# Feed-forward key products in f32r parts, and a new plan for the side work of an attention loop

## The reference

```python
x = L0_attn_x                                     # 4 x 2048 x 256, f32
# attention, 16 heads of 16, 16 "splats" a head
qkv = layernorm(x) @ qkv_w.T
w(t) = exp(sum((t - centers)**2) * inv_var)       # for q and for k, per splat
logits = einsum(w(q), w(k), amplitudes) / temp
x = x + (softmax(logits) @ v) @ out_w.T
# feed-forward
h = layernorm(x); h_prev = h shifted by one token
xr = mu_r * h + (1 - mu_r) * h_prev;  xk = mu_k * h + (1 - mu_k) * h_prev
r = sigmoid(xr @ W_r.T)
k_act = square(relu(xk @ W_k.T))
x = x + r * (k_act @ W_v.T)
```

## Time and profile before

| | |
|---|---|
| median of 3 runs | 2138.8 us (2138.59 to 2140.33) |
| the profiled execution, its own time | 2140.03 us |
| its span in the trace | 2138.2 us |
| PE / PE weight loads busy | 2108.5 us (99%) / 947.4 us (44%) |
| ACT busy | 2003.9 us (94%) |
| DVE busy | 822.9 us (38%) |
| POOL busy | 398.1 us (19%) |
| first and last exponential start | 46.9 and 2103.4 us |

### The profile page before, as it was taken

One profiled execution on the slowest core, in us unless ns is written; L12 is line 12 of the kernel. 1 busy time (PEld: TensorE's weight loads), 2 busy tenths in 40 slices (PEclk: granted clock), 3 DMA queues, 4 the chain that ended last, 5 costly groups with the idle time before them and its releaser, 6 DMA issues.

```text
span 2138.2 us, 52139 instructions
## 1 busy us (share of the span) xinstructions
PE 2108.5 (99%) x22756; PEld 947.4 (44%) x22756; DVE 822.9 (38%) x1886; ACT 2003.9 (94%) x2184; POOL 398.1 (19%) x502
## 2 busy tenths in 40 slices
PE   7999999999999999999999999999999999999999
PEld 4444444444444444444444444444444444443445
DVE  6123433332436252524425225262244334514236
ACT  4999999999999999999999999999999999999995
POOL 0243342424242020220402202204000000000000
PEclk9999999999999999999999999999999999999999
DMA  6534444436533315124241421612422141221111
GB/s 196 140 94 124 120 130 127 122 90 169 126 113 98 73 61 156 34 89 118 73 136 44 125 83 49 164 36 76 110 58 55 40 90 41 44 63 34 34 41 45
DMA packets 176489, 193.59 MB, mean 91 GB/s; under 512 B 88656, under 2 KB 108496, under 8 KB 176240
## 3 DMA queue, kind: packets, MB, share of 16 engines
q1 hardware_dynamic: 166720, 174.69, 29.4%
q0 software_dynamic: 7424, 15.22, 2.9%
q10 hardware_dynamic: 2096, 0.14, 0.1%
HBM read 98.90 MB, written 75.81 MB: 82 GB/s over the span
## 4 chain that ended last, share of the span: by engine, by line
PE 79%; ACT 17%; DVE 3%; issue 1%; DMA 0%; DVEq 0%; ACTq 0%
PE ps_pv L1000 35%; PE ps_scores L981 24%; PE ps_step L1028 16%; ACT probs L1325 15%; PE ps_step L1049 1%; DVE h_t L1675 1%; ACT weight L1385 1%; PE ps_scores L1018 0%; PE ps_scores L1013 0%; PE ps_scores L1176 0%; DVE mixed_r L1660 0%; PE ps_scores L1022 0%; DMA x_prep<-x 0%; ACT gate L1382 0%; DVE gate_in L1628 0%
## 5 line engine op out<-in xcount | busy, mean ns | idle before, releaser
L1325 ACT ACTIVATE probs<-ps_scores 128x1024 f32<-128x1024 f32 x2048 | 1938.1, 1037 | 82.2 <-PE ps_scores L981 54.1
L1000 PE MATMUL ps_pv<-probs,vals 128*32 128x512 f32 (+5 forms) x9760 | 1071.8, 531 | 1.1 <-DVE o_raw L1690 1.1
L981 PE MATMUL ps_scores<-q_aug,k_aug 49*128 49x512 f32 x4096 | 707.3, 439 | 11.8 <-ACT probs L1325 7.8
L981 PEld LDWEIGHTS ps_scores<-q_aug,k_aug 49*128 49x128 f32 x4096 | 331.6, 184 | 635.5 <-ACT probs L1325 591.6
L1000 PEld LDWEIGHTS ps_pv<-probs,vals 128*32 128x32 f32 x9760 | 335.8, 139 | 208.7 <-issue 121.0
L1443 POOL DMA_DIRECT2D packed<-qk x232 | 116.9, 509 | 830.3 <-DVE qk L1617 802.7
L1448 POOL TENSOR_TENSOR packed<-qk 32x512 f32<-32x512 f32 x232 | 246.9, 1064 | 17.5
L1453 POOL TENSOR_TENSOR k_act<-k_act 128x512 f32<-128x512 f32 x28 | 29.1, 1040 | 825.0 <-DVE k_act L1620 825.0
L1690 DVE COPY o_raw<-ps_pv 128x512 f32<-128x512 f32 x63 | 43.6, 691 | 266.2 <-PE ps_pv L1000 266.0
L1617 DVE COPY qk<-ps_step 128x512 f32<-128x512 f32 x58 | 40.0, 690 | 216.6 <-PE ps_step L1028 216.4
L1620 DVE TENSOR_SCALAR k_act<-ps_step 128x512 f32<-128x512 f32 x29 | 20.0, 691 | 236.9 <-PE ps_step L1028 236.9
(11 more groups left out here) (217 smaller groups left out, 1101.7 us busy)
## 6 DMA issues: line engine op xcount, KB each, us to landing
k_aug<-k_parts SPq DMA_DIRECT2D x128, 192.0 KB, 4.6
q_aug<-q_parts SPq DMA_DIRECT2D x128, 192.0 KB
k_parts<-parts SPq DMA_DIRECT2D x31, 512.0 KB, 3.2
q_parts<-parts SPq DMA_DIRECT2D x31, 512.0 KB, 3.2
packed<-qk POOLq DMA_DIRECT2D x232, 64.0 KB, 2.2
x_ffn<-x SPq DMA_DIRECT2D x18, 512.0 KB, 5.3
vals<-v_kept SPq DMA_DIRECT2D x64, 128.0 KB, 5.2
k_parts<-parts SPq DMA_DIRECT2D x31, 256.0 KB, 3.4
```

What stands on the lines that cost most here:

```text
L981: mm = pe.matmul(ps_scores[:, g % RING, e, :], k_aug[rows, s % 2, pair, kt * P:(kt + 1) * P], q_aug[rows, u % 2, pair, :], start=True, sto ...
L1000: mm = pe.matmul(ps_pv[32 * c:32 * c + 32, at], vals[:, s % 2, kt, :, c], probs[:, tick % PROB_SLOTS, c, at], start=(kt == 0), stop=(kt == ...
L1325: act.activation(probs[:, tick % PROB_SLOTS, 2 * pair:2 * pair + 2, :], ps_scores[:, g % RING, :, :], ACT.Exp).then_inc(probs_ready, 1)
```

## The change

It makes five edits.

1. `k0` and `k1` of the feed-forward (14 chunks in the loop) are no longer f32 products in quarters. Both operands are split into a high part (rounded to f32r) and a low part (the rest, f32r), and the product is the sum of three f32r products: high by high, low by high, high by low. A piece is now one matmul of 128 rows, 128 columns of weights and 512 columns, 3 terms by 2 halves: 6 pieces instead of 8.
2. In a gap, pieces of `k1`, and of `k0` other than those that begin it, run directly behind the scores, ahead of all values.
3. DVE gets two operations more for each half of `mixed_k` (cast and subtraction), and two for the weights once. `MIX` grows by 4.
4. `wk_high` and `wk_low` are new tiles; `unit_row` lies in `wk_low`, `mixed_k_high` in `shift`, and `mixed_k` shares its memory with `mixed_k_low`.
5. The numbers of the plan change.

```diff
-NORM_AHEAD = 8
+NORM_AHEAD = 9
-RATE = 1.45
+RATE = 1.34
 RATE_FIRST = 1.5
-RATE_UNTIL = 96
-RATE_LATE = 2.0
+RATE_UNTIL = 140
+RATE_LATE = 3.2
 RATE_FROM = 930
-MOST = 3.5
+MOST = 4.5
-BONUS = 0
+BONUS = 0.5
...
-URGENT = 0
+URGENT = 2
...
-             begun(task, "r0") if part < 2 else begun(task, "k0"), 5, (task, part))
+             begun(task, "r0") if part < 2 else begun(task, "k0"), 5 if part < 2 else 11, (task, part))
...
-def pieces_of(name):
+def pieces_of(task, name):
+    if task[0] == "ffn" and name in ("k0", "k1"):
+        return TERMS * HALVES
     return 4 if name.startswith("dist") else 8
...
-        unit_row = sb("unit_row", [1, CHUNK], F32R)
...
+        unit_row = wk_low[0:1, :, :].rearrange("p a n -> p (a n)")
+        mixed_k_high = shift
...
                 if name == "k0" and first == 0:
                     pe.wait_ge(mix_steps, MIX * (n + 1))
+                    if n == 0:
+                        pe.wait_ge(wk_split, 2)
...
                 elif name.startswith("k"):
-                    mm = columns_in_quarters(wk, index * P, mixed_k, first, last)
+                    for part in range(first, last + 1):
+                        half, term = divmod(part, TERMS)
+                        lhs, rhs = ((wk_high, mixed_k_high), (wk_low, mixed_k_high), (wk_high, mixed_k_low))[term]
+                        mm = pe.matmul(ps_step[:, :], lhs[:, half, index * P:(index + 1) * P], rhs[:, half, :],
+                                       start=(part == 0), stop=(part == TERMS * HALVES - 1))
...
+            def in_terms(task, name, first, last):
+                return task[0] == "ffn" and (name == "k1" or name == "k0" and first > 0)
...
                 ahead, behind = ([], values_in(gap)) if gap % 2 else (values_in(gap)[:-1], values_in(gap)[-1:])
+                work = work_in(gap)
+                while work and in_terms(*work[0]):
+                    task, name, first, last = work.pop(0)
+                    ffn_piece(task, name, first, last)
                 for tick, slices in ahead:
                     values(tick, slices)
-                for task, name, first, last in work_in(gap):
+                for task, name, first, last in work:
...
+                if which:
+                    if FFN_NO[task] == 0:
+                        v.wait_ge(shifts_stored, 16 * NB * HALVES)
+                    v.wait_ge(mix_steps, n.total())
+                    v.tensor_copy(mixed_k_high[:, half, :], mixed_k[:, half, :]).then_inc(mix_steps, n.step())
+                    v.wait_ge(mix_steps, n.total())
+                    v.tensor_tensor(mixed_k_low[:, half, :], mixed_k[:, half, :], mixed_k_high[:, half, :].bitcast(F32),
+                                    ALU.subtract).then_inc(mix_steps, n.step())
+
+            def split_weights():
+                v.wait_ge(ffn_weights_loaded, 16 * 12)
+                v.wait_ge(ones_loaded, 16 * 2)
+                v.tensor_copy(wk_high[:, :, :], wk[:, :, :]).then_inc(wk_split, 1)
+                v.wait_ge(wk_split, 1)
+                v.tensor_tensor(wk_low[:, :, :], wk[:, :, :], wk_high[:, :, :].bitcast(F32), ALU.subtract).then_inc(wk_split, 1)
```

More of the change, by code:

```diff
@@ L240, in lay_side_work @@
         if now and gap % 2 == 0:
-            room = min(room, share_of(gap, pair, (pieces_of(now[1]) - now[2]) / 2))
+            room = min(room, share_of(gap, pair, (pieces_of(*now[:2]) - now[2]) / 2))
         while now and room > 0:
@@ L248, in lay_side_work @@
             now = task, name, part + 1
-            if part + 1 == pieces_of(name):
+            if part + 1 == pieces_of(task, name):
                 order.append((task, name))
@@ L493 @@
 DUTY_AT = pace_duties()
+WK_SPLIT_AT = next(tick for tick in itertools.count(KT * NC) if not any(
+    tick + ahead in found for ahead in range(4) for found in (EVICT_AT, *DUTY_AT.values())))
 def load(gap):
@@ L560, in preln_block @@
         wk = sb("wk", [P, HALVES, D])
+        wk_high = sb("wk_high", [P, HALVES, D], F32R)
+        wk_low = sb("wk_low", [P, HALVES, D], F32R)
         wv = sb("wv", [P, HALVES, D])
@@ L607, in preln_block @@
         mixed_r = sb("mixed_r", [P, HALVES, CHUNK])
-        mixed_k = sb("mixed_k", [P, HALVES, CHUNK])
+        with nc.sbuf_tensor("mixed_k", [P, HALVES, CHUNK], F32) as mixed_k:
+            pass
+        mixed_k_low = sb("mixed_k_low", [P, HALVES, CHUNK], F32R)
         tmp = sb("tmp", [P, 2, CHUNK])
@@ L706, in preln_block @@
         mix_steps = sem("mix_steps")
+        wk_split = sem("wk_split")
         k_squared = sem("k_squared")
@@ L722, in preln_block @@
         TURNED = 1 + 4 * TT
-        MIX = TURNED + 8
+        MIX = TURNED + 12
         MAX_TILES = KT * (HEADS * NC + 1)
@@ L841, in _ @@
                 sp.dma_start(out=rows.rearrange("p (n t) -> p n t", t=CHUNK),
-                             in_=unit_row[:, :].bitcast(F32).unsqueeze(1).broadcast_to([1, 4 * NC, CHUNK])).then_inc(ones_loaded, 16)
+                             in_=unit_row.bitcast(F32).unsqueeze(1).broadcast_to([1, 4 * NC, CHUNK])).then_inc(ones_loaded, 16)
             for to, of in ((wout, out_wT), (wr, r_wT), (wk, k_wT), (wv, v_wT)):
@@ L1077, in prep_piece @@
                     mm = columns_in_quarters(wqkv, cols, src, first, last)
-                if last == pieces_of(name) - 1:
+                if last == pieces_of(task, name) - 1:
                     mm.then_inc(step_mm, 1)
@@ L1677, in mix @@
             def mix(task, part):
-                n = Count(MIX * FFN_NO[task] + TURNED + 2 * part)
+                n = Count(MIX * FFN_NO[task] + TURNED + (0, 2, 4, 8)[part])
                 which, half = divmod(part, 2)
@@ L1732, in _ @@
             v.wait_ge(unit_set, 1)
-            v.tensor_copy(unit_row[:, :], tmp[0:1, 0, :]).then_inc(unit_set, 1)
+            v.tensor_copy(unit_row, tmp[0:1, 0, :]).then_inc(unit_set, 1)
             v.wait_ge(x_loaded, 16)
@@ L1846, in _ @@
                     late_split(task, half, side)
+                if tick == WK_SPLIT_AT:
+                    split_weights()
             n = FFN_NO[LAST]
```

## The result

The changed kernel takes 2151.93 us (median, 2149.17 to 2152.66), the kernel before 2139.36 in the same comparison: ratio 1.0057, interval 1.0045 to 1.0068. It is slower by 12.6 us or 0.6%, where 2141 was forecast with a range up to 2149. The profiled execution took 2149.17 us with a span of 2147.3.

What follows compares the result with a forecast made beforehand. PE was taken as the bound, ACT having about half a microsecond a pair to spare. Terms summed +5+0-6+4 = +3 us on the profiled 2140.03 us; 2141 us was stated, as some lost pairs may vanish, range 2126 to 2149.

Steps and rivals of the forecast that it cites:

- thin pairs: Loop pairs of 5 pieces, where a piece costs 0.13 of its 0.216 us: +6 us of PE time taken as +5.
- (2): New key pieces on PE: 168 whole-array f32r matmuls at 0.236 us each, +3.4 us.
- (3): One more change of array shape behind scores, 0.22 us in 63 gaps: +13.9 us, and +1 for pieces between values.
- Rival A: Changing from scores to the whole array costs nothing: 2127 us; chance 0.30, shared with side-work order removing more stalls.
- (1): Key products in the loop: 56 pieces fewer at 0.216 us each, 12.1 us less PE time.
- (5): Plan's middle part: slower rate, at most 6 pieces a pair plus BONUS, fewer dense pairs: -6 us.
- (6): Plan's last 27 pairs: 9 pieces a pair allowed instead of 7, more pairs empty: +4 us, bounds 0 and +9.
- Step (4): Added casts and subtractions on DVE, 35 us in sum, hidden beneath other work: 0, bounds -4 and +6 us.
- Rival C: DVE's split comes late for k0, 14 x 0.7 = +10 us, 2151 us; chance 0.13.
- Rival B: Last part bunches to 9 pieces a pair, +9 us there, late key gaps add 0.3 each: 2148 us; chance 0.17.
- Rival D: ACT is the bound, so the change saves nothing: 2139 us; chance 0.40 together with the forecast itself.
- (7): Tiles `unit_row`, `shift` and `mixed_k_low` only share memory: 0 us.

Runs made afterwards that it cites:

- experiment 9: Changed kernel with key pieces as f32 quarter matmuls, six of eight done, so a quarter of each key product left out: 2138.57 us, ratio 0.9993.
- experiment 2: Kernel before, f32 key products in quarters kept, with only the seven new numbers of the plan: 2146.33 us, ratio 1.0033.
- experiment 10: The changed kernel itself timed again, nothing changed, beside other follow-up runs: 2149.43 us, ratio 1.005.
- experiment 13: Changed kernel with a plan levelled by piece counts (RATE_LATE 2.0, RATE_FROM 942, MOST 3.0, BONUS 0): 2156.36 us, ratio 1.0082.
- experiment 7: Changed kernel with RATE_LATE 2.0 and MOST 3.5 as before, the rest of the new plan kept: 2147.57 us, ratio 1.004.

## Why the prediction was wrong

Of the whole, +10.9 us in the stretches: shapes and f32r +13.0, the stall +3.4, and the remainder (six pieces instead of eight, and the plan) -5.5. The prediction had +18.3, 0 and -14.1, with 1 us taken off for thin pairs.

**Steps (2) and (3), the new pieces and the shapes: mechanism right, size too high.** Predicted +3.4 +13.9 +1 = 18.3 of PE time, measured 13.0 of span. The prices in a gap were right to 0.01 us or so: 0.232 between key matmuls (0.236 taken), 0.323 for the change (0.09 of standstill), 0.337 to the second (0.10 of weights), 0.326 to the values (0.09 again). The gaps are 58, not 63, which gives 58 x 0.22 + 3.4 = 16 us on PE. The missing 3 us are in the middle: by experiment 9 the four late pairs, with six pieces and two key gaps, pay the full price of 0.60, but middle pairs of three and three pieces, also six, only 0.27, pairs of three and two 0.15, and two pairs with three or four pieces nothing. So it isn't thin pairs alone. That it is ACT which hides the rest is argued from the slope of the earlier trace rows, not shown. Rival A, a free change, is refuted by the gaps and by experiment 9. The rule that the prediction cited from the Trainium skill (TensorEngine Tiling (Array Packing), Key Properties), that a change of mode drains the engine, agrees with the trace in this fourth direction: 0.323 against a pitch of 0.232.

**Steps (1), (5) and (6) together: the failed step.** They are the sum "-12.1, -6, +4" = -14.1; experiment 9 against before, without the stall, gives 1211.04-1217.62 = -6.6 in the middle and 183.93-182.89 = +1.0 late, -5.5. The prediction was 8.6 us too hopeful here, its largest error. The step that fails is pricing 56 removed pieces at PE's full 0.216 each and then adding the levelling of the same pairs on top. By the plan's own counts 53 of the 56 pieces leave the middle, and removal and levelling together brought 6.6 us there, 0.12 a piece. That is near the 0.13 that the prediction had read from the earlier trace rows as the price of a piece in a pair of 4 to 6; it took off only 1 us for it, and from the net of (1) to (3).

The terms aren't additive, and the runs show it in both orders. Under the new numbers the removal is there: from experiment 2 to 9, -2.3 in the middle and -10.2 late, -12.4 without the stall, as (1) has it. But then the new numbers by themselves, on eight pieces, cost +6.9 (experiment 2), where (5) and (6) have -2. Under the old numbers the removal is nearly nothing: 12.35 us for the change without the stall, less 13.06 for the shapes, is -0.7, with 19 empty pairs by the plan's own counts where there were 9. (This is an estimate across plans, since the 13.06 were measured under the new numbers, with 58 key gaps instead of 62.) Then the new numbers are worth -7.0 in the middle and +2.2 late. A plan that deals out a fixed rate with less work per task makes pairs about as dense and leaves more of them empty, at ACT's floor; the slower rate is what turns removed pieces into time. So no single one of the three is the wrong one; their sum is.

A part stays open. The new counts of the middle (99 pairs of five pieces instead of 67, 80 of six instead of 101, none of seven instead of 13), priced at the mean lengths of such pairs before (5.90, 6.12 and 6.51), give -12.9, where (1) and (5) had -18.1 and -6.6 was measured. The rest of 6.3 is mainly that pairs of six take 6.19 us in the mean in experiment 9 and 6.12 before; no run shows why.

**Step (4), the split on DVE: predicted 0 (-4 to +6), measured +3.4**, all of it one stall at a place that the prediction didn't name. It looked at `k0`, which waits for the split, and found cover; that was right: the only wait of PE in front of a key matmul in the trace of after is 0.5 us, for an eviction. What was queued behind the added operations on DVE was another duty, the copy of a unit's values, and PE waits for that one. Rival C had DVE late fourteen times at 0.7; it was once, at 3.4 (1.3 of it clock), and for another consumer. Rival B (+9 late) was too high: +3.4 late, of which 2.4 are shapes. Rival D, ACT as the bound, was put into the forecast; it is half true, as the 0.12 us of a removed piece show.

**(7)** and the tail: nothing found; from the start of the last score matmul to the end it is 36.1 us, against 36.0 before.

So the sum was short by 8.6 (removal, levelling and the late part added up) and 3.4 (stall), and 5.3 too high in the shapes (18.3 against 13.0), or 4.3 when the 1 us taken off is counted: 5+0-6+4 = 3 was predicted, 3+8.6+3.4-4.3 = 10.7, and 10.9 measured. The medians gave 10.7 (experiment 10) to 12.6.

## What to carry to other kernels

Where a planner deals out side work at a fixed rate, work taken away saved time only together with a lower rate, and then once; price the plan that results, by its pairs, not the removed pieces, and expect a part of it to turn on which duty falls before which copy. Fewer instructions in another shape of the array must save more than the changes of shape cost: here six pieces instead of eight save 2 x 0.216 = 0.43 us a product at most on PE and enter 58/28 = 2.1 gaps, at 0.22 each 0.46, so it doesn't pay. And an operation added to an in-order engine is to be held against everything queued behind it, above all what frees a PSUM bank, not only against its own consumer.

## What the runs showed of the hardware that was not expected

**DVE beside POOL.** POOL ran four tensor products in after from 690.85 on:

```profile
690.85 4.84 POOL L1472 TENSOR_TENSOR packed<-qk 32x512 f32<-32x512 f32 x4
```

Beside them DVE's 128x512 operations from SBUF took 1.28 (scaling), 1.41 (multiply-add), 1.08 (cast) and 1.41 us (subtraction), where the same four took 0.49, 0.75, 0.43 and 0.69 at 1339 us in experiment 13, with no POOL product beside them. Over the whole trace of after it is the same: 25 of the 28 casts of `mixed_k` have no POOL product beside them and take 0.43 to 0.52 us, the three that have one 1.08 to 1.15. The copies out of PSUM at 0.69 don't change. The added split is thus 1.1 us where POOL is idle and 2.5 where it isn't. The Trainium skill (GPSIMD Engine Reference, Specifications) says that the two share SBUF interfaces, with contention when a DVE instruction is in a 2-port performance mode or has two SBUF inputs. The multiply-add and the subtraction have two such inputs, and their durations agree; in which mode the scaling and the cast ran, no trace shows.

**The clock behind the stall.** PE stood idle from about 694.9 to 696.9 in after, and the granted clock fell behind it:

```profile
696.00:697.00 1.00, 0.06 (x4) 1.00 1.03 287
697.00:698.00 1.00, 1.00 (x8) 0.74 0.36 67
698.00:699.00 1.00, 1.00 (x8) 0.50 0.00 0
```

It was at 0.5, the lower of its two levels, while PE was fully busy again. In experiment 7 the same stall wasn't followed by a fall, and the stretch took 14.05 us instead of 15.33: the stall by itself costs 2.1 and the clock 1.3, and up to 0.4 more in the middle (1221.73 against 1221.30), since the clock was still at 0.50 when the stretch ended.
